# Keys of 41 chunks turned in 32 x 32 blocks on VectorE and by a trip through device memory, in an attention-and-FP4-feed-forward kernel for one core

## The reference, cut to what matters

```python
# x: (16, 512, 256); 16 heads of 64; FFN width 704
q, k, v = split_heads(ln(x) @ Wq), split_heads(ln(x) @ Wk), split_heads(ln(x) @ Wv)
q, k = relu(q) + 0.001, relu(k) + 0.001
context = cumsum(einsum('bhnd,bhne->bhnde', k, v), axis=2)      # causal linear attention
D_inv   = 1 / einsum('bhnd,bhnd->bhn', cumsum(k, axis=2), q)
attn    = einsum('bhnd,bhnde,bhn->bhne', q, context, D_inv)
x = x + attn @ Wo + bo
h = silu(fp4(ln(x)) @ fp4(w_gate).T) * (fp4(ln(x)) @ fp4(w_up).T)   # FP4 in blocks of 16
x = x + fp4(h) @ fp4(w_down).T
```

## Time and profile before

| what | value |
|---|---|
| median of 3 runs | 1522.74 us |
| profiled execution | span 1522.3 us from first to last instruction; the page names no other time for it |
| PE busy | 1491.0 us (98%) |
| VectorE (DVE) busy | 1183.0 us (78%) |
| ScalarE (ACT) busy | 650.7 us (43%) |
| GpSimd (POOL) busy | 725.2 us (48%) |
| 16 DMA engines, mean | about 29%, 88 GB/s |

### The profile page before, as it was taken

How to read it: one execution, slowest core, us unless ns; L and a number is a source line. 1 busy time by engine, 2 the same in 40 slices (tenths; PEclk the granted TensorE clock), 3 DMA queues, 4 the chain that set the end, 5 groups by cost and what they waited for, 6 DMA issues and landing times.

```text
span 1522.3 us, 55070 instructions
## 1 busy us (share of the span) xinstructions
PE 1491.0 (98%) x23652; PEld 1401.0 (92%) x23652; DVE 1183.0 (78%) x2322; ACT 650.7 (43%) x1165; POOL 725.2 (48%) x822
## 2 busy tenths in 40 slices
PE   8889999999999999999999999999999999999998
PEld 7878999999999999999999999999999999999998
DVE  8786777877878877778777778777778877878767
ACT  5434444343453444443343443444443343453433
POOL 4313555444555444554444554445554444554543
PEclk9999999999999999999999999999999999999999
DMA  4101233233233333233333233232233232233210
GB/s 168 34 2 43 85 102 109 77 97 95 83 104 100 88 95 96 77 110 92 89 103 92 85 105 96 86 102 86 84 113 101 79 103 89 81 112 92 82 51 15
DMA packets 159361, 133.27 MB, mean 88 GB/s; under 512 B 12944, under 2 KB 150672, under 8 KB 159120
## 3 DMA queue, kind: packets, MB, share of 16 engines
q1 hardware_dynamic: 159120, 129.75, 28.6%
HBM read 68.09 MB, written 61.60 MB: 85 GB/s over the span
## 4 chain that ended last, share of the span: by engine, by line
PE 81%; DVE 5%; DMA 3%; issue 2%; SPq 1%; ACT 1%; POOL 1%; DVEq 0%; POOLq 0%; ACTq 0%
PE bank L607 62%; PE bank L740 3%; PE bank L808 3%; PE bank L729 3%; PE bank L774 3%; PE bank L691 2%; DMA hq_away<-hq_blocks 1%; DMA attn_away<-probs 1%; PE bank L835 1%; PE bank L855 1%; PE bank L617 1%; PE bank L713 1%; PE bank L886 1%; SPq L563 0%; DVE probs L1835 0%
## 5 line engine op out<-in xcount | busy, mean ns | idle before, releaser
L1517 POOL TENSOR_TENSOR attnT_lo<-attn,attnT_hi 128x1024 fp32r<-128x1024 f32 x58 | 141.2, 2434 | 253.2 <-ACT attnT_hi L1200 253.2
L607 PE MATMUL bank<-xT_hi,wqk_hi 128*128 128x256 f32 x1024 | 211.1, 287 | 2.8 <-ACT qkT L1127 1.5
L607 PE MATMUL bank<-xT_hi,wqk_lo 128*128 128x256 f32 x1024 | 203.6, 280 | 0.0
L607 PE MATMUL bank<-xT_lo,wqk_hi 128*128 128x256 f32 x1024 | 203.4, 280 | 0.0
L1127 ACT ACTIVATE qkT<-bank 128x512 f32<-128x512 f32 x256 | 149.7, 595 | 113.6 <-PE bank L607 110.9
L1577 POOL TENSOR_SCALAR qkT<-qkT 128x512 f32<-128x512 f32 x256 | 158.4, 632 | 61.8 <-ACT qkT L1127 60.7
L607 PEld LDWEIGHTS bank<-xT_hi,wqk_hi 128*128 128x128 f32 x1024 | 157.1, 188 | 7.2 <-issue 3.8
L607 PEld LDWEIGHTS bank<-xT_lo,wqk_hi 128*128 128x128 f32 x1024 | 156.5, 188 | 0.0
L607 PEld LDWEIGHTS bank<-xT_hi,wqk_lo 128*128 128x128 f32 x1024 | 156.5, 188 | 0.0
L1250 ACT ACTIVATE silu<-bank 128x352 f32<-128x352 f32 x128 | 58.7, 459 | 222.5 <-PE bank L607 221.0
L1529 POOL TENSOR_TENSOR hqT_lo<-hq,hqT_hi 128x768 fp32r<-128x768 f32 x58 | 130.7, 2253 | 17.8 <-ACT hqT_hi L1215 17.6
(11 more groups left out here) (219 smaller groups left out, 3868.4 us busy)
## 6 DMA issues: line engine op xcount, KB each, us to landing
attn<-attn_away SPq DMA_DIRECT2D x232, 128.0 KB, 2.9
hq_away<-hq_blocks SPq DMA_DIRECT2D x58, 384.0 KB, 3.2
hq<-hq_away SPq DMA_DIRECT2D x232, 96.0 KB, 2.3
attn_away<-probs SPq DMA_DIRECT2D x58, 256.0 KB, 2.7
attn_away<-probs SPq DMA_DIRECT2D x116, 128.0 KB, 2.7
x_in<-in_L_attn_x SPq DMA_DIRECT2D x32, 256.0 KB, 2.8
out<-out_sb SPq DMA_DIRECT2D x64, 128.0 KB, 2.7
qkT<-in_L_attn_Wq SPq DMA_DIRECT2D x1, 1024.0 KB, 8.4
```

The lines of the kernel that those rows point to most:

```text
L607: at = pe.matmul(dst, lhs_at(kt), rhs_at(kt), start=first and kt == 0, stop=last and kt == k_tiles - 1)
L1517: pool.tensor_tensor(by_raw_attn(attnT_lo), attn_raw, by_raw_attn(attnT_hi).bitcast(F32), ALU.subtract).then_inc(attnT_ready, 2)
```

## The change

The keys of 41 chunks (g = 8 to 61 without the last chunk of each sequence; `SENT_KEYS`) no longer pass PE and ACT. At the end of an odd step DVE turns the 32 x 32 blocks of the keys of the next one or two chunks from `qkT` into the first 1024 columns of `probs` (`block_keys`, after c = 3 two chunks, after c = 1 one). SP writes the blocks to `keys_away` in device memory (`send_keys`, one DMA of 512 KB) and reads them back into `k_tok` in two parts of four DMAs of 64 KB each (`fetch_keys` for the half that `early_keys` reads, `fetch_late_keys` for the other). The masks of the even step that follows wait until the last block tile is written out (`keys_sent`). `turn_k` and `keys_to_tokens` stay for the other seven chunks that have them. Four more edits come along: in units 4 to 30 the four key tiles are projected before the four query tiles (`KEYS_FIRST`), so scores wait for 6 of 8 tiles at first where they waited for 4; the CAST of `low_x` becomes a subtraction that reads PSUM; POOL does `scale_x(g - 2)` ahead of `low_sent_attn(g - 1)` in odd steps; and on DVE `begin_h` of odd steps is split around `end_x` and `add_early` (for c = 1 both now come before the scaling). SP's order in odd steps changes too.

```diff
+    SENT_KEYS = [g for g in range(2 * CHUNKS, END) if g % CHUNKS < CHUNKS - 1]
+    EARLY_K_UNITS = range(SENT_KEYS[0] // HALF, END // HALF)
+        KEYS_FIRST = [4, 5, 6, 7, 0, 2, 1, 3]
...
+        def keys_turned_in(g):
+            if g % 2 == 0:
+                return []
+            return [n for n in (g + 1, g + 2) if n in SENT_KEYS]
...
 # SP
+            def send_keys(n):
+                k = n % CHUNKS
+                sp.wait_ge(key_blocks_ready, sent_keys(n) + 1)
...
+                sp.dma_start(keys_away[k], key_blocks).then_inc(keys_sent, 16)
+            def fetch_keys(n):
+                c = n % CHUNKS
+                sp.wait_ge(keys_sent, 16 * (sent_keys(n) + 1))
+                sp.wait_ge(kv_early_done, (CHUNKS - 1) * (n // CHUNKS) + c)
+                for j, (to, at) in enumerate(key_groups(n)):
+                    h = key_part(j, False)
+                    sp.dma_start(to[:, h], at[:, h]).then_inc(keys_back, 16)
...
                 if c % 2 == 0:
...
+                    if g in SENT_KEYS:
+                        fetch_late_keys(g)
+                    if c == 0 and g + 1 in SENT_KEYS:
+                        fetch_keys(g + 1)
...
                 else:
+                    if c == 1 and g in SENT_KEYS:
+                        fetch_late_keys(g)
                     if g - 3 in SENT_HQ:
                         send_hq(g - 3)
-                        fetch_hq(g - 3)
                     if g in SENT_ATTN:
                         send_attn(g)
-                        fetch_attn(g)
+                    if g - 3 in SENT_HQ:
+                        fetch_hq(g - 3)
                     if exists(g - 4, END - 4):
                         store(g - 4)
+                    if g in SENT_ATTN:
+                        fetch_attn(g)
+                    for k, n in enumerate(keys_turned_in(g)):
+                        send_keys(n)
+                        if k == 0:
+                            fetch_keys(n)
 # PE
-                pe.wait_ge(qk_ready, PAIRS * u + 4)
+                pe.wait_ge(qk_ready, half_of_qk(u))
...
+                    if g in SENT_KEYS:
+                        pe.wait_ge(keys_back, 16 * GROUPS * (sent_keys(g) + 1))
...
-                    turn_k(b, c, g)
+                    if g not in SENT_KEYS:
+                        turn_k(b, c, g)
 # POOL, odd_step
-                low_sent_attn(g - 1)
                 if is_late(g - 2):
                     scale_x(g - 2)
+                low_sent_attn(g - 1)
 # DVE
-                dve.wait_ge(xT_ready, 2 * u + 1)
-                dve.tensor_copy(lo[:, :, P:3 * DH], lo[:, :, 0:DH].bitcast(F32)).then_inc(xT_ready, 1)
+                low(lo[:, :, P:3 * DH], got[:, :, 0:DH], hi[:, :, 0:DH], xT_hi_ready, 2 * u + 1, xT_ready)
...
+                if n == 0 and g % 2 == 0 and keys_turned_in(g - 1):
+                    dve.wait_ge(keys_sent, 16 * sent_keys(keys_turned_in(g - 1)[-1] + 1))
...
+            def block_keys(n, first):
+                t, u = n % HALF, n // HALF
+                if first:
+                    dve.wait_ge(qk_ready, PAIRS * u + PAIRS // 2)
+                    dve.wait_ge(attn_sent, 48 * sent_attn(n))
+                else:
+                    dve.wait_ge(keys_sent, 16 * sent_keys(n))
+                dve.transpose(key_blocks.rearrange("p (j h c q) -> p h q j c", j=GROUPS, h=2, c=GROUP),
+                              qkT[:, PAIRS:2 * PAIRS, t * P:(t + 1) * P].rearrange("p (h q) (j c) -> p h q j c", h=2, c=GROUP)
+                              ).then_inc(key_blocks_ready, 1)
...
                 gated_by_silu(g - 2, 1)
+                turned = keys_turned_in(g)
+                if turned:
+                    block_keys(turned[0], True)
                 begin_h(g - 2)
+                if len(turned) > 1:
+                    block_keys(turned[1], False)
```

More of the change, by code:

```diff
@@ L564, in fetch_attn, with key_groups, key_part, fetch_late_keys @@
                                  ).then_inc(attn_back, 16)
+            def send_keys(n):
+                k = n % CHUNKS
+                sp.wait_ge(key_blocks_ready, sent_keys(n) + 1)
+                if n - CHUNKS in SENT_KEYS:
+                    sp.wait_ge(keys_back, 16 * GROUPS * (sent_keys(n - CHUNKS) + 1))
+                    sp.wait_ge(late_keys_back, 16 * GROUPS * (sent_keys(n - CHUNKS) + 1))
+                sp.dma_start(keys_away[k], key_blocks).then_inc(keys_sent, 16)
+            def key_groups(n):
+                at = keys_away[n % CHUNKS].rearrange("(a r) (j h e) -> j r h a e", r=GROUP, j=GROUPS, h=2)
+                to = k_tok[:].rearrange("p (h a e) -> p h a e", h=2, a=GROUPS)
+                return [(to[GROUP * j:GROUP * (j + 1)], at[j]) for j in range(GROUPS)]
+            def key_part(j, late):
+                return int((j >= GROUPS // 2) != late)
+            def fetch_keys(n):
[5 more added lines that the diff above has]
+                    sp.dma_start(to[:, h], at[:, h]).then_inc(keys_back, 16)
+            def fetch_late_keys(n):
+                sp.wait_ge(kv_done, (CHUNKS - 1) * (n // CHUNKS) + n % CHUNKS)
+                for j, (to, at) in enumerate(key_groups(n)):
+                    h = key_part(j, True)
+                    sp.dma_start(to[:, h], at[:, h]).then_inc(late_keys_back, 16)
             def store(n):
@@ L613, in turn_x @@
                 pe.wait_ge(xn_ready, u + 1)
-                k = banks.take(pe, ("x", unit_place(u, 0), 0), b, xT_ready, lambda b: 2 * (UNITS * b + c // 2 + 1) + 1 if c != "first" else 1)
+                k = banks.take(pe, ("x", unit_place(u, 0), 0), b, xT_ready, lambda b: 2 * (UNITS * b + c // 2 + 2) if c != "first" else 2)
                 for kt in range(KD):
@@ L730, in turn_k, with keys_of, keys_by_values @@
                     last.then_inc(k_turned, 1)
-            def keys_by_values(c, kv, late):
+            def keys_of(g, rows, pair, odd):
+                if g in SENT_KEYS:
+                    h, q = divmod(pair, HALF_PAIRS)
+                    at = k_tok[:].rearrange("p (h o d q) -> p h o q d", h=2, o=2, d=DH)
+                    return at[rows, h, odd, q, :]
+                at = pair * P + DH * odd
+                return k_tok[rows, at:at + DH]
+            def keys_by_values(g, kv, late):
+                c = g % CHUNKS
                 for j in range(HALF_PAIRS):
@@ L1335, in even_step @@
                     square_h(g - 3)
-                for n in range(2):
-                    keys_to_tokens(b, c, n)
+                if g not in SENT_KEYS:
+                    for n in range(2):
+                        keys_to_tokens(b, c, n)
                 high_xq(g - 2)
@@ L1349, in odd_step @@
                 g, u = CHUNKS * b + c, UNITS * b + c // 2
-                if c < CHUNKS - 1:
+                if c < CHUNKS - 1 and g not in SENT_KEYS:
                     for n in range(2):
```

51 lines of the change are left out of this document (37 added, 14 removed).

## The result

The kernel after takes 1562.4 us (median of 4 runs, 1558.51 to 1564.97), that of before beside it 1524.12 us (4 runs, 1522.6 to 1529.41): a ratio of 1.0237 with a 95% interval of 1.0219 to 1.0255. It is slower by 2.4%, outside the forecast range and on the other side of no change. The profiled execution took 1558.51 us, 36 more than that of before.

The account below looks back on a forecast made before the run. PE, busy 98% of the span, was taken as the bound. 1522.3 - 37.0 (transposes) - 2.7 (present waits) + 16 (stalls at c = 0) = 1498.6, stated as 1500 us, 1.5% faster; range 1482 to 1530.

Parts of the forecast that it names:

- What is added to engines: DVE gets 41 block transposes at 1.22 us, 3.7 us a sequence, no bound; CAST's replacement and PE's first wait cost nothing.
- a rule on transposes: Trainium skill: transpose 128 x 128 on TensorE if the result may go to PSUM; VectorE only turns 32 x 32 blocks.
- What is removed: PE's key transposes in 41 chunks, 0.85 to 0.93 us each: 37.0 us; ACT's 82 copies, 49 us, nothing by themselves.
- the slots: PE's start-to-start times of a chunk's removed transposes: 0.93 us for c = 0 and 2, 0.85 for c = 1.
- The chain from c = 3 into c = 0: Two key tiles pass one buffer before the masks of c = 0; masks 1.1 to 1.2 us late, 14 times: 16 us.
- The stall: PE's wait for late masks at L774 or L808 in each of 14 steps with c = 0: 1.1 to 1.2 us.
- The rest: CAST replaced by a PSUM read, POOL's scale_x first, scores waiting for 6 of 8 tiles: costed at nothing.
- the chain takes more than it gives: Rival, chance 0.21: one buffer and SP's queue make c = 0 stalls cost over 39.7 us; 1532 at 3.5 us landings.
- the signs that the prediction named for a term wrongly set to nothing: PE waiting for keys_back at early_keys or attnT_lo at project_out, or DVE late at the products.
- The page's rule: By it the change loses: PE transposes a chunk in 0.93 us, DVE in 1.22 plus two landings of 2.3 or more.

Follow-up runs that it names:

- e2_stride: Kernel before, with ACT writing k_tok with four pairs interleaved and PE reading keys with a step of four, nothing else: 1565.14 us, 1.0264.
- e1_unit: Kernel after, but the state update reads sent keys with a step of one (wrong columns, only time counts): 1537.27 us, 1.0073.
- e9_own_unit: Kernel after with two own tiles for the turned keys and keys read with a step of one (wrong output): 1490.9 us, 0.978.
- the square: Four kernels, one shared or two own key tiles: step of four 1562.4 (after) and 1523.3 us, step of one 1537.3 and 1490.9 us.
- e6_own: Kernel after, step of four kept, with two own tiles for the turned keys, so masks wait for no send (wrong output): 1523.33 us, 0.9972.
- e4_rest: Kernel after with no chunk's keys sent, all 48 transposes on PE, the four other edits kept: 1519.94 us, 0.9968.
- e3_unit_blocks: Kernel after with keys read at a step of one and DVE writing its blocks without interleaving (wrong output): 1538.91 us, 1.0104.
- e7_c12: Kernel after, but only the 27 chunks c = 1 and 2 sent, one tile at a time, step of four kept: 1522.6 us, 0.9979.
- e10_step2: Kernel after, but only 27 chunks (c = 1, 2) sent, scattered in runs of 64 elements, two heads interleaved, read at step two: 1502.3 us, 0.9848.
- e5_stride2: Kernel before, with k_tok written with two heads interleaved and keys read with a step of two: 1526.27 us, 0.9997.

## Why the prediction was wrong

**Two steps failed**, and either one alone takes the gain away. The first is the list of what is added: under "What is added to engines" the prediction prices DVE's transposes, the CAST and a wait, and nothing for PE. It takes over keys by values from before as if its instructions were the same. They are the same in number and shape, but 41 chunks read their stationary operand with a step of four: 41 x 0.98 = 40 us, more than the 37.0 that were removed. e2_stride shows this cost in the kernel before (40 us), and e1_unit and e9_own_unit show it go: in the square it is worth 25 us where PE also waits for the masks, and 32 us where it doesn't. The Trainium skill has the rule (Advanced Engine Details and Errata, SBUF Cachelines): a 16-byte line needs at least two hits for full speed. Four fp32 elements are one line, so a step of four hits each line once and a step of two twice; the runs agree, with 210 ns for a load at four and 135 at two. The prediction weighed a rule on transposes and did not ask how the result is read. The second is the size of the chain: priced at 16 us, it costs 39 us with the step of four (after against e6_own) and 46 us without it (e1_unit against e9_own_unit).

**What is removed** nearly held in the steps, less so over the whole run. Against e4_rest, e9_own_unit has the c = 2 step at 0.93 us less, c = 1 at 0.79 (0.85) and c = 0 at 0.62 (0.93): 2.42 us a sequence where the slots say 2.71. The 0.31 us at c = 0 are what is left for the added traffic and DVE's work; no run isolates them. The whole run gains 29 us and not 37.0: the thirteen sequences give 31.5 of 35.2, the stretch ahead of chunk 8 is 2.5 us longer (222.1 us against 219.6), and the last sequence gives nothing.

**The chain from c = 3 into c = 0** was the right mechanism at the right place, mis-sized. On the mean the masks start 4.4 us behind scores, not 2.6: the first send is 0.9 us late, the second 1.3, and its landing takes 3.3 us instead of 2.8. Most of the lateness of the sends is SP's issuing: I took 1.74 and 1.73 us for four reads from the one step in the earlier trace rows, and in the kernel after four reads take 1.7 to 3.1 us. The transposes of 2.07 us, where the earlier trace rows said 1.22 of one whose output is not interleaved, are an error of the forecast that the path hardly felt (e3_unit_blocks). The masks were needed at 772.97, or 1.5 us behind scores, and 1.6 is when they start in e9_own_unit, where nothing holds them. The stall was forecast at 1.15 us. By the wait rows it is 23.2 / 14 = 1.7 us; by step lengths, the median c = 0 step of 16.83 us against 14.77 in e6_own, 2.06: 29 us instead of 16. The full 1.8 us by which the masks are later does not show, in part since the slower keys by values brings PE there 0.5 us later. Without the step of four it does: e1_unit has 16.82 us against 13.87 in e9_own_unit, 2.95 us a step.

**The clock** was in no term. c = 0 steps average 0.7 us above their median, 10 us in 14, and the windows show them at the lower level. e6_own, e7_c12 and e9_own_unit, without the stalls, have 0.998 again. e6_own's 39 us are this and the stall: 29 + 10.

**The rest** (CAST, POOL's order, keys first), costed at nothing, gains 4 to 5 us. The row L1742 for x did fall as said, in the mean from 1366 to 419 ns as L1827, and the CAST's 1178 ns became 412; that is 85 us of DVE, and PE's wait for the state copy at c = 0 is 0.4 us in e4_rest where it was 2.7. Which of the edits brings it was not tried singly.

Sum, on the profiled spans: 1522.3 - 37.0 + 40 + 29 + 10 - 5 = 1559; measured 1556.8. The rival "the chain takes more than it gives" was given 0.21 and a time of 1532. e1_unit is its kernel, the one tile and no step of four, and takes 1537 us: that rival was right in its mechanism and nearly in its price, and had left out the step of four like the rest. Had the chain been priced rightly at 16 us and only the step of four been missed, the time would be e6_own's 1523 plus 16, also above before. So the direction was wrong for two reasons, each of them enough. Of the signs that the prediction named for a term wrongly set to nothing, the list of waits has one of 0.9 us for `attnT_lo`, once, and no other: a slower weight load is no wait, and stands in no list of waits. The page's rule was right in its verdict for this kernel and not for the reason: e10_step2 transposes 27 chunks by the other way and gains 1.5%.

Why did e9_own_unit gain 32 us on e6_own where the slots say 40? The shortest steps of the two differ by 0.98, 1.01 and 0.98 us (c = 0, 1, 2), as the slots have it. But e9_own_unit has more long ones: with c = 0 they reach 15.33 us where the shortest takes 13.79, so that the means differ by 0.86, 0.84 and 0.84 only. In e2_stride it was 0.80 to 1.23. What holds up the long ones is open.

## What to carry to other kernels

When work moves to another path, price the consumer too: write down the access pattern in which each engine reads and writes the new copy, and find a row with that same step, not just the same shape. A buffer that two transfers pass through in turn before it is needed has a price in every round, here 2 to 3 us a time, and the waits can drag down TensorE's clock on top. Two defects that hide each other (PE slow, so it waits less) are only told apart by removing both.

## What the hardware showed

- A weight load of 64 x 64 fp32 took 134 ns at a step of one, 135 at two and 210 (the mean of e2_stride) at four elements. A group of 32 such loads with their matmuls took 0.52 us of TensorE at a step of one and 1.01 at four.
- A block transpose of 128 x 1024 fp32 on VectorE took 1.22 to 1.24 us with its output at a step of one or two, 2.07 at four. ScalarE's copy of 128 x 512 from PSUM took 594 ns, 633 with its output at a step of two (e5_stride2) and 1127 at four (e2_stride).
- TensorE's clock fell to its lower level in four of the 14 steps with c = 0 of the kernel after: in those where the first wait was 1.15 to 1.89 us. It did not fall where the first wait was at most 0.67 us and a second of 1.03 us followed, nor behind the single wait of 1.03 us at 884.63.
